# A transformer block on eight cores: the last LayerNorm's apply goes from VectorE to GpSimd, and four weight reads become one

## The chip, the cores and the metric

The kernel runs on 8 cores of one Trainium2 chip. Each core works on one sequence of the batch; nothing is exchanged between cores, and all read their own copy of the same weights. The metric is the device time of the slowest core in microseconds, from a run of the whole kernel. A profile is of one execution; its own time is given beside its span.

## The reference, cut to what matters

```
# per core: x is one sequence, 4096 tokens of 1024
h  = LN(x, g1, b1); spec = h @ W_to.T                # 1024 -> 512
scan over tokens: (sr, si) = clip(rotate(decay*(sr,si) + 0.1*(real,imag)))
x2 = x + 0.1 * (scan_out @ W_from.T)                 # 512 -> 1024
h  = gelu(LN(x2, g3, b3) @ W1.T + b1f)               # 1024 -> 4096
x3 = x2 + 0.1 * (h @ W2.T + b2f)                     # 4096 -> 1024
y  = LN(x + x3)
# eight experts, each token uses the two with the highest router logits
out = LN(y + sum_e c_e * ((silu(y @ G_e.T) * (y @ U_e.T)) @ D_e.T))
```

All LayerNorms are over the 1024 features. The last two have no gain and no bias. Every expert is computed for every token; c_e is zero for those not chosen.

## The kernel before

The data lies transposed: features on the 128 partitions, in KC = 8 chunks, and T = 512 tokens along the row. The sequence is worked in NT = 8 tiles of 512 tokens; `xc(buf, k)` is chunk k of a buffer, 128 x 512. X0 holds the tile's input, X2 the residual stream, ACC the float32 sum of the experts' outputs, BFIN0 and BFIN1 the bf16 inputs of the matmuls.

**Order.** Every engine has one list of instructions that is written out by the Python loops in program order, and it runs it in this order. `w(eng, ms)` puts a wait for a semaphore value into a list; `opi` and `opd` append an instruction or a DMA and return the value that it will raise. VectorE has a drain behind each instruction. SyncE's list holds all the large DMAs: a wait there holds back every DMA behind it.

**Per tile i.** LN3 from X2 (`emit_ln`), feed-forward layer 1 in eight slabs of weights (`emit_ffn1`, matmuls L660), layer 2 in eight slabs (`emit_ffn2`, L693), the LayerNorm to y with `twopass=True`, the router, and then the loop over the eight experts, with four slabs for gate and up (L834) and two for down (L874) each. ACC starts as y, written by GpSimd in eight steps (L458 and L460, `p2_step`) that are strewn over the expert loop, together with the first part (`make_chain`) of tile i + 1.

**The final LayerNorm.** What is done with ACC when the experts are through is a closure, `make_p2`. It isn't run at once, but in `emit_ffn1` of the next tile, behind slab fr = 3; for the last tile it runs at the end. It calls `emit_ln` with ACC: ScalarE casts eight chunks (L408), TensorE sums them with a matrix of ones (L413), ScalarE squares (L417), TensorE sums (L422), VectorE makes MEANT and the variance (L429 to L434), ScalarE takes the root (L436), VectorE the reciprocal into RSTD (L438). Then the apply: for each chunk a subtraction of MEANT (L470, into ZS) and a multiplication with RSTD (L472, back into ACC). Behind it SyncE waits for the last of them (L892) and issues eight output DMAs (L894). MEANT and RSTD are single buffers, which every LayerNorm writes. `st["p2_done"]` is the end of GpSimd's L460 steps, which also read MEANT and RSTD; VectorE waits for it at L432.

**Slabs.** A slab is 128 x 4096 bf16 (1 MB), in one of the four slots of RING (`ring_slot`). In tiles 1 to 7 it is loaded with one DMA from a scratch copy in memory (`emit_slab_load`, L384), as soon as SyncE reaches it and the slot is free. In tile 0 the scratch copy doesn't exist yet. Then `prepass_unit` reads the float32 weights into two slots, 1 MB each (L264), VectorE casts the first half (L295) and ScalarE the second (L293) into a third slot, SyncE waits for both casts and writes the slot to the scratch copy (L299), and TensorE uses the same slot. There are 64 slabs: 8 of w1, 8 of w2, 32 of gate and up, 16 of down. `prepass_unit` also brings in W_to and W_from at the start. Rows of the float32 weights in memory are 16 KB apart for w1T, 4 KB for w2T and dpT and 8 KB for guT; one read takes 2 KB out of each of 128 rows.

Of the kernel before, what the change touches and what calls it, by code (L numbers as in the profile page):

```python
# [8 lines left out]
F32 = mybir.dt.float32  # L9
# [7 lines left out]
KC = D // 128  # L17
# [13 lines left out]
def build(stop_stage="full"):  # L31
# [34 lines left out]
    with es:  # L66
# [14 lines left out]
        G = sb("G", [128, 32 * T], BF16)  # L81
        SG = sb("SG", [128, 8 * T], BF16)
        MEANT = sb("MEANT", [128, T])
        RSTD = sb("RSTD", [128, T])
# [35 lines left out]
        def w(eng, ms):  # L120
            if ms is None:
                return
            if isinstance(ms, list):
                for m in ms:
                    w(eng, m)
                return
            sk, v = ms
            q[eng].append(lambda E, s=sems[sk], vv=v: E.wait_ge(s, vv))
# [28 lines left out]
        bank_free = [None] * 8  # L157
        bank_ready = [None] * 8
# [18 lines left out]
        def slot_dma(j, fn):  # L177
            return opd("sync", "R%d" % j, fn)
# [76 lines left out]
        def prepass_unit(srcs, dst_sb=None, dst_dram=None, scale=None, ncols=2048):  # L255
            halves = []
            for hv in range(len(srcs)):
                jj, slot, msf = ring_slot()
                w("sync", msf)
                g = srcs[hv].shape[0]  # L260
                gc_ = ncols // g
                ms_rd = None
                for gg in range(g):
                    ms_rd = slot_dma(jj, lambda E, d=slot.bitcast(F32)[:, gg * gc_:(gg + 1) * gc_], s=srcs[hv][gg]: E.dma_start(out=d, in_=s))  # L264
                halves.append((jj, slot, ms_rd))
            CENG = (("vector", "V"), ("scalar", "S"))
            if dst_sb is not None:
                ms_cs = []
                for hv, (jj, slot, ms_rd) in enumerate(halves):
                    eng, sk = CENG[hv % 2]  # L270
                    w(eng, ms_rd)
                    dstap = dst_sb[:, hv * ncols:(hv + 1) * ncols]
                    if eng == "scalar":
                        ms_c = opi(eng, sk, lambda E, d=dstap, s=slot.bitcast(F32)[:, 0:ncols], sc=(scale or 1.0): E.activation(out=d, in_=s, func=AF.Copy, scale=sc))
                    elif scale is None:
                        ms_c = opi(eng, sk, lambda E, d=dstap, s=slot.bitcast(F32)[:, 0:ncols]: E.tensor_copy(out=d, in_=s))
                    else:
                        ms_c = opi(eng, sk, lambda E, d=dstap, s=slot.bitcast(F32)[:, 0:ncols], sc=scale: E.tensor_scalar(out=d, in0=s, scalar1=sc, scalar2=None, op0=OP.mult))
                    ring_set_free(jj, ms_c)
                    ms_cs.append(ms_c)  # L280
                return ms_cs, None
            jo, oslot, msfo = ring_slot()
            ms_cs = []
            for hv, (jj, slot, ms_rd) in enumerate(halves):
                eng, sk = CENG[hv % 2]
                w(eng, ms_rd)
                if hv == 0:
                    w(eng, msfo)
                else:
                    w(eng, msfo)  # L290
                dstap = oslot[:, hv * ncols:(hv + 1) * ncols]
                if eng == "scalar":
                    ms_c = opi(eng, sk, lambda E, d=dstap, s=slot.bitcast(F32)[:, 0:ncols]: E.activation(out=d, in_=s, func=AF.Copy))  # L293
                else:
                    ms_c = opi(eng, sk, lambda E, d=dstap, s=slot.bitcast(F32)[:, 0:ncols]: E.tensor_copy(out=d, in_=s))  # L295
                ring_set_free(jj, ms_c)
                ms_cs.append(ms_c)
            w("sync", ms_cs)
            ms_wr = slot_dma(jo, lambda E, d=dst_dram, s=oslot[:]: E.dma_start(out=d, in_=s))  # L299
            return ms_cs, ms_wr, jo, oslot  # L300
# [87 lines left out]

        def emit_ln(src, bfin_p, gv=None, bv=None, dstf=None, out_bf=True,
                    src_ready=None, extra_swait=None, extra_twait=None, extra_vwait=None,  # L390
                    twopass=False):
            BFIN = BFINS[bfin_p]
            per_chunk = isinstance(src_ready, list) and len(src_ready) == KC
            if not per_chunk:
# [4 lines left out]
            sq_ms = [None] * KC  # L399
# [26 lines left out]
            if twopass:  # L426
                bfin_user[bfin_p] = None
            w("vector", bank_ready[0])
            opi("vector", "V", lambda E: E.tensor_scalar(out=MEANT[:], in0=PB[0][:], scalar1=float(1.0 / D), scalar2=None, op0=OP.mult))  # L429
            opi("vector", "V", lambda E: E.tensor_tensor(out=ZS[:, 0:T], in0=MEANT[:], in1=MEANT[:], op=OP.mult))  # L430
            w("vector", bank_ready[1])
            w("vector", st.get("p2_done"))  # L432
            opi("vector", "V", lambda E: E.scalar_tensor_tensor(out=PB[1][:], in0=PB[1][:], scalar=float(1.0 / D), in1=ZS[:, 0:T], op0=OP.mult, op1=OP.subtract))
            ms_veps = opi("vector", "V", lambda E: E.tensor_scalar(out=PB[1][:], in0=PB[1][:], scalar1=float(EPS), scalar2=None, op0=OP.add))  # L434
            w("scalar", ms_veps)
# [7 lines left out]
            if twopass:  # L443
                st["p1_stats"] = ms_pow

                def pass1():
                    for k in range(KC):
                        opi("vector", "V", lambda E, k=k: E.tensor_tensor(out=ZS[:, 0:T], in0=src(k), in1=MEANT[:], op=OP.subtract))
                        bf_ms[k] = opi("vector", "V", lambda E, k=k: E.tensor_tensor(out=xc(BFIN, k), in0=ZS[:, 0:T], in1=RSTD[:], op=OP.mult))  # L449
                    bank_free[0] = bf_ms[KC - 1]  # L450
                    bank_free[1] = bf_ms[KC - 1]
                st["p1_pass1"] = pass1

                def p2_step(k):
                    def go():
                        if k == 0:
                            w("gpsimd", [extra_vwait, bf_ms[KC - 1]])
                        ms_sub = opi("gpsimd", "G", lambda E, k=k: E.tensor_tensor(out=dstf(k), in0=src(k), in1=MEANT[:], op=OP.subtract))  # L458
                        w("gpsimd", ms_sub)
                        f_ms[k] = opi("gpsimd", "G", lambda E, k=k: E.tensor_tensor(out=dstf(k), in0=dstf(k), in1=RSTD[:], op=OP.mult))  # L460
                        st["p2f_%d" % k] = f_ms[k]
                        if k == KC - 1:
                            st["p2_done"] = f_ms[k]
                    return go
                st["p1_pass2_steps"] = [p2_step(k) for k in range(KC)]
                st["p1_sq"] = sq_ms
                return cast_ms, None, sq_ms[KC - 1], bf_ms, f_ms
            w("vector", extra_vwait)
            for k in range(KC):
                opi("vector", "V", lambda E, k=k: E.tensor_tensor(out=ZS[:, 0:T], in0=src(k), in1=MEANT[:], op=OP.subtract))  # L470
# [14 lines left out]
        st = {}  # L485

        def make_chain(j):
# [57 lines left out]
            steps.append(s_ln1a)  # L545

            def s_ln1b():
                w("vector", [bank_ready[0], st.get("p2_done")])
                opi("vector", "V", lambda E: E.tensor_scalar(out=MEANT[:], in0=PB[0][:], scalar1=float(1.0 / D), scalar2=None, op0=OP.mult))
                opi("vector", "V", lambda E: E.tensor_tensor(out=ZS[:, 0:T], in0=MEANT[:], in1=MEANT[:], op=OP.mult))  # L550
                w("vector", bank_ready[1])
                w("vector", st.get("p2_done"))
                opi("vector", "V", lambda E: E.scalar_tensor_tensor(out=PB[1][:], in0=PB[1][:], scalar=float(1.0 / D), in1=ZS[:, 0:T], op0=OP.mult, op1=OP.subtract))
                ms_veps = opi("vector", "V", lambda E: E.tensor_scalar(out=PB[1][:], in0=PB[1][:], scalar1=float(EPS), scalar2=None, op0=OP.add))
                w("scalar", ms_veps)
                ms_sqr = opi("scalar", "S", lambda E: E.activation(out=PB[1][:], in_=PB[1][:], func=AF.Sqrt))
                w("vector", ms_sqr)
                ms_rec = opi("vector", "V", lambda E: E.reciprocal(out=RSTD[:], in_=PB[1][:]))
                bank_free[1] = ms_rec
                ms_pow = ms_rec  # L560
# [156 lines left out]
        for i in range(NT):  # L717
# [170 lines left out]
            def make_p2(i=i, t0=t0, acc_ms=list(acc_ms), gu_ms=last_gu_mm[0]):  # L888
                def p2():
                    _, ms_out, _, _, _ = emit_ln(lambda k: xc(ACC, k), i % 2, dstf=lambda k: xc(ACC, k), out_bf=False,  # L890
                                                 src_ready=acc_ms[KC - 1], extra_swait=gu_ms)
                    w("sync", ms_out)  # L892
                    for k in range(KC):
                        opd("sync", "SO", lambda E, k=k, t0=t0: E.dma_start(out=outTr[k, :, t0:t0 + T], in_=xc(ACC, k)))  # L894
                    prev_out_so[0] = ("SO", cnt["SO"])
                return p2
# [64 lines left out]
```

How the kernel before makes its waits and increments, by code:

```python
        def w(eng, ms):  # L120
            if ms is None:
                return
            if isinstance(ms, list):
                for m in ms:
                    w(eng, m)
                return
            sk, v = ms
            q[eng].append(lambda E, s=sems[sk], vv=v: E.wait_ge(s, vv))
# [8 lines left out]
        def opi(eng, sk, fn):  # L137
            cnt[sk] += STEP[sk]
            v = cnt[sk]
            q[eng].append(lambda E, fn=fn, s=sems[sk], st=STEP[sk]: fn(E).then_inc(s, st))
            if eng in DRAIN_ENGS:
                q[eng].append(lambda E: E.drain())
            return (sk, v)
# [1 line left out]
        def opd(eng, sk, fn):  # L145
            cnt[sk] += STEP[sk]
            v = cnt[sk]
            q[eng].append(lambda E, fn=fn, s=sems[sk], st=STEP[sk]: fn(E).then_inc(s, st))
            return (sk, v)
```

## Time and profile before

| | us |
|---|---|
| runs of the kernel | 5863.69 and 5514.01, median 5688.85 |
| the profiled execution, its own time | 5507.56 |
| its span on the slowest core (core 1) | 5506.0 |
| spans of the eight cores | 5481.4 to 5506.0 |
| TensorE busy (matmuls) | 4188.6, 76% |
| VectorE busy | 1987.8, 36% |
| ScalarE busy | 1045.9, 19% |
| GpSimd busy | 468.8, 9% |
| memory traffic | read 625.09 MB, written 83.89 MB |

Engines are printed as PE (TensorE's matmuls), PEld (its weight loads), DVE (VectorE), ACT (ScalarE), POOL (GpSimd) and SP (SyncE); a q behind a name is its instruction queue, where DMA issues stand. L and a number is a line of the kernel. Times are microseconds from the span's start, the mean of one instruction in ns where it says so. Tile 0 reaches to about 1150 us, the seven others take some 620 us each. What released a waiting instruction is inferred from semaphores: where several were waited for, the one that came last is named.

### The profile page before, as it was taken

How to read it: one execution, taken by the hardware profiler on the slowest of the kernel's cores; microseconds unless marked ns; L12 is line 12 of the kernel's file. 1: busy time of each engine (PE TensorE's matmuls, PEld its weight loads, DVE VectorE, ACT ScalarE, POOL GpSimd, SP SyncE). 2: the span in 40 equal slices, each digit the busy share in tenths (PEclk: the TensorE clock that was granted, in tenths of full speed). 3: DMA queues.
4: the chain of work that ended last, by engine and by line, in shares of the span. 5: the costliest groups of instructions: out<-in, count | busy, mean ns of one | idle time of the engine just before them, and what ended most of it. 6: DMA issues, size and time to landing. Idle time of an engine off the chain costs nothing.

```text
span 5506.0 us, 56606 instructions; the slowest of 8 cores (5481.4 to 5506.0 us)
## 1 busy us (share of the span) xinstructions
PE 4188.6 (76%) x18088; PEld 1776.7 (32%) x18088; DVE 1987.8 (36%) x2937; ACT 1045.9 (19%) x1560; POOL 468.8 (9%) x398
## 2 busy tenths in 40 slices
PE   1365666667899688977899588976899588976897
PEld 0122222223343233433334233433334233433343
DVE  4313442232443235332443235332443235332333
ACT  1122212231111221121101221121201221121111
POOL 0001000000201010100201010100201010100210
PEclk9687888878999789988999789988899789988998
DMA  2265566634233233314233233314234233323342
GB/s 62 66 229 194 201 209 239 238 121 153 107 123 138 84 115 115 138 69 153 107 120 141 82 117 109 143 70 153 100 123 144 80 120 109 138 76 138 115 144 94
DMA packets 178013, 712.66 MB, mean 129 GB/s; under 512 B 28609, under 2 KB 28737, under 8 KB 112194
## 3 DMA queue, kind: packets, MB, share of 16 engines
q1 hardware_dynamic: 168770, 708.95, 36.3%
q8 instruction: 158, 2.59, 0.2%
q10 hardware_dynamic: 8960, 0.10, 0.1%
q14 instruction: 125, 1.02, 0.1%
HBM read 625.09 MB, written 83.89 MB: 129 GB/s over the span
## 4 chain that ended last, share of the span: by engine, by line
PE 63%; DVE 17%; DMA 5%; ACT 5%; SPq 4%; issue 3%; DVEq 1%; ACTq 1%; POOL 0%; POOLq 0%
PE PB L834 28%; PE PB L874 15%; PE PB L660 8%; PE PB L693 7%; SPq L264 3%; DMA RING<-guT 2%; DVE ZS L470 2%; ACT RING L293 2%; DVE RSTD L438 1%; DVE UPE L847 1%; PE PB L633 1%; DVEq L142 1%; DVE PRD L853 1%; DMA RING<-scr_w 1%; PE PB L413 1%
## 5 line engine op out<-in xcount | busy, mean ns | idle before, releaser
L834 PE MATMUL PB<-BFIN,RING 128*128 128x512 bf16 x8192 | 1893.2, 393 | 222.1 <-ACT RING L293 108.8
L834 PEld LDWEIGHTS PB<-BFIN,RING 128*128 128x128 bf16 x8192 | 815.1, 100 | 1280.9 <-issue 392.3
L874 PE MATMUL PB<-PRD,RING 128*128 128x512 bf16 x4096 | 968.6, 399 | 223.3 <-DVE PRD L853 139.9
L660 PE MATMUL PB<-BFIN,RING 128*128 128x512 bf16 x2048 | 514.2, 413 | 440.2 <-DMA RING<-scr_w 225.2
L847 DVE TENSOR_TENSOR UPE<-PB,CBE 128x512 f32<-128x512 f32 x512 | 354.0, 691 | 997.7 <-PE PB L834 960.1
L874 PEld LDWEIGHTS PB<-PRD,RING 128*128 128x128 bf16 x4096 | 411.3, 102 | 775.5 <-issue 351.4
L880 DVE TENSOR_TENSOR ACC<-PB,ACC 128x512 f32<-128x512 f32 x512 | 353.9, 691 | 685.5 <-PE PB L874 666.7
L853 POOL TENSOR_TENSOR PRD<-SG,UPE 128x512 bf16<-128x512 bf16 x256 | 297.1, 1161 | 2799.7 <-DVE UPE L847 2728.2
L841 ACT ACTIVATE SG<-PB 128x512 bf16<-128x512 f32 x512 | 303.6, 597 | 1033.8 <-PE PB L834 1028.0
L693 PE MATMUL PB<-G,RING 128*128 128x512 bf16 x2048 | 465.8, 386 | 21.1 <-ACT RING L293 13.3
L660 PEld LDWEIGHTS PB<-BFIN,RING 128*128 128x128 bf16 x2048 | 211.8, 104 | 741.4 <-issue 539.1
L693 PEld LDWEIGHTS PB<-G,RING 128*128 128x128 bf16 x2048 | 197.5, 99 | 272.6 <-issue 53.8
L703 DVE SCALAR_TENSOR_TENSOR X<-PB,X 128x512 f32<-128x512 f32 x64 | 44.3, 692 | 652.5 <-PE PB L693 652.3
L458 POOL TENSOR_TENSOR ACC<-X,MEANT 128x512 f32<-128x512 f32 x64 | 82.8, 1295 | 2084.4 <-DVE BFIN L449 2084.4
L817 ACT ACTIVATE CBE<-PB 128x512 f32<-128x512 f32 x64 | 38.2, 597 | 1141.8 <-PE PB L814 1140.7
L666 ACT ACTIVATE G<-PB,BHV 128x512 bf16<-128x512 f32 x256 | 175.9, 687 | 276.0 <-PE PB L660 275.7
L853 DVE TENSOR_TENSOR PRD<-SG,UPE 128x512 bf16<-128x512 bf16 x256 | 187.6, 733 | 60.9 <-DVE UPE L847 60.3
L293 ACT ACTIVATE RING<-RING 128x2048 bf16<-128x2048 f32 x64 | 122.2, 1909 | 381.7 <-DMA RING<-dpT 161.8
L295 DVE CAST RING<-RING 128x2048 bf16<-128x2048 f32 x64 | 81.1, 1267 | 297.9 <-DMA RING<-guT 96.0
L408 ACT ACTIVATE BFIN<-X 128x512 bf16<-128x512 f32 x128 | 74.0, 623 | 444.8 <-DVE X L706 394.6
L429 DVE TENSOR_SCALAR MEANT<-PB 128x512 f32<-128x512 f32 x24 | 16.6, 691 | 311.6 <-PE PB L413 311.6
L633 PE MATMUL PB<-ZB,WFR 128*128 128x512 bf16 x256 | 77.3, 431 | 60.5 <-DVE STI L621 51.6
(134 smaller groups left out, 1837.4 us busy)
## 6 DMA issues: line engine op xcount, KB each, us to landing
RING<-scr_gu SPq DMA_DIRECT2D x224, 1024.0 KB, 4.9
RING<-scr_w SPq DMA_DIRECT2D x112, 1024.0 KB, 4.9
RING<-scr_dp SPq DMA_DIRECT2D x112, 1024.0 KB, 4.8
RING<-guT SPq DMA_DIRECT2D x256, 256.0 KB, 5.3
scr_gu<-RING SPq DMA_DIRECT2D x32, 1024.0 KB, 4.9
RING<-dpT SPq DMA_DIRECT2D x128, 256.0 KB, 5.1
X<-xT SPq DMA_DIRECT2D x64, 256.0 KB, 5.3
RING<-w1T SPq DMA_DIRECT2D x64, 256.0 KB, 6.7
```

Of the source, the lines that this page charges most:

```text
L264: ms_rd = slot_dma(jj, lambda E, d=slot.bitcast(F32)[:, gg * gc_:(gg + 1) * gc_], s=srcs[hv][gg]: E.dma_start(out=d, in_=s))
L293: ms_c = opi(eng, sk, lambda E, d=dstap, s=slot.bitcast(F32)[:, 0:ncols]: E.activation(out=d, in_=s, func=AF.Copy))
L633: mmm = opi("tensor", "T", lambda E, c=c, oc=oc: E.matmul(PB[7][:], WFR[:, c * 1024 + oc * 128: c * 1024 + (oc + 1) * 128], xc(ZB, c), sta ...
L660: mmm = opi("tensor", "T", lambda E, k=k, fc4=fc4, b=b, slot=slot: E.matmul(PB[b][:], slot[:, k * 512 + fc4 * 128: k * 512 + (fc4 + 1) * 1 ...
L666: g_ms[fc] = opi("scalar", "S", lambda E, b=b, fc=fc: E.activation(out=xc(G, fc), in_=PB[b][:], func=AF.Gelu, bias=BHV[:, fc:fc + 1]))
L693: mm_last = opi("tensor", "T", lambda E, jx=jx, kr=kr, oc4=oc4, b=b, slot=slot: E.matmul(PB[b][:], slot[:, jx * 512 + oc4 * 128: jx * 512 ...
L834: mmm = opi("tensor", "T", lambda E, k=k, fc4=fc4, b=b, slot=slot, BFIN=BFIN: E.matmul(PB[b][:], slot[:, k * 512 + fc4 * 128: k * 512 + (f ...
L841: sg_ms[gc] = opi("scalar", "S", lambda E, b=b, gc=gc: E.activation(out=xc(SG, gc), in_=PB[b][:], func=AF.Silu))
L847: ms_up = opi("vector", "V", lambda E, b=b, par=par: E.tensor_tensor(out=xc(UPE, par), in0=PB[b][:], in1=CBE[:], op=OP.mult))
L853: prev_upe[par] = opi(peng, psem, lambda E, uc=uc, par=par: E.tensor_tensor(out=xc(PRD, uc), in0=xc(SG, uc), in1=xc(UPE, par), op=OP.mult))
L874: mmm = opi("tensor", "T", lambda E, k=k, oc4=oc4, b=b, slot=slot: E.matmul(PB[b][:], slot[:, k * 512 + oc4 * 128: k * 512 + (oc4 + 1) * 1 ...
L880: acc_ms[oc] = opi("vector", "V", lambda E, oc=oc, b=b: E.tensor_tensor(out=xc(ACC, oc), in0=PB[b][:], in1=xc(ACC, oc), op=OP.add))
```

## The change

Two things are changed. In `prepass_unit`, the g reads of 128 rows x 2 KB of one half become a single DMA whose access patterns have three levels: partition, row block k, column. Bytes, source, destination and slot are the same, and the semaphore is waited for at the value of one DMA in place of g. g is 4, for W_from 2.

In `emit_ln` there is a new path, `apply_gp`, which only the final LayerNorm takes. GpSimd waits for the reciprocal and then does subtraction and multiplication of the eight chunks in place in ACC, each multiplication behind a wait for its own subtraction. Its end is kept as `pl2_done`, and VectorE waits for it, and for `p2_done`, ahead of each new MEANT; the wait for `p2_done` that stood ahead of L433 is now ahead of L429.

```diff
@@ prepass_unit
-                ms_rd = None
-                for gg in range(g):
-                    ms_rd = slot_dma(jj, lambda E, d=slot.bitcast(F32)[:, gg * gc_:(gg + 1) * gc_], s=srcs[hv][gg]: E.dma_start(out=d, in_=s))
+                dview = slot.bitcast(F32)[:, 0:ncols].rearrange("p (k f) -> p k f", k=g)
+                sview = srcs[hv].rearrange("k p f -> p k f")
+                ms_rd = slot_dma(jj, lambda E, d=dview, s=sview: E.dma_start(out=d, in_=s))
@@ emit_ln
             w("vector", bank_ready[0])
+            w("vector", [st.get("p2_done"), st.get("pl2_done")])
             opi("vector", "V", lambda E: E.tensor_scalar(out=MEANT[:], ...
             opi("vector", "V", lambda E: E.tensor_tensor(out=ZS[:, 0:T], ...
             w("vector", bank_ready[1])
-            w("vector", st.get("p2_done"))
...
+            if apply_gp:
+                w("gpsimd", [ms_rec, extra_vwait])
+                for k in range(KC):
+                    m1 = opi("gpsimd", "G", lambda E, k=k: E.tensor_tensor(out=dstf(k), in0=src(k), in1=MEANT[:], op=OP.subtract))
+                    w("gpsimd", m1)
+                    f_ms[k] = opi("gpsimd", "G", lambda E, k=k: E.tensor_tensor(out=dstf(k), in0=dstf(k), in1=RSTD[:], op=OP.mult))
+                st["pl2_done"] = f_ms[KC - 1]
+                bank_free[0] = f_ms[KC - 1]
+                bank_free[1] = f_ms[KC - 1]
+                return None, f_ms[KC - 1], sq_ms[KC - 1], bf_ms, f_ms
@@ s_ln1b, the first LayerNorm of the next tile
-                w("vector", [bank_ready[0], st.get("p2_done")])
+                w("vector", [bank_ready[0], st.get("p2_done"), st.get("pl2_done")])
@@ make_p2
-                                                 src_ready=acc_ms[KC - 1], extra_swait=gu_ms)
+                                                 src_ready=acc_ms[KC - 1], extra_swait=gu_ms, apply_gp=True)
```

## Rows read from the trace of the kernel before

**Rows 1.** The chain that ended last: shares by engine (page), by line

```profile
PE 63%; DVE 17%; DMA 5%; ACT 5%; SPq 4%; issue 3%; DVEq 1%; ACTq 1%; POOL 0%; POOLq 0%
...
by line: PE PB L834 28.4%; PE PB L874 14.9%; PE PB L660 7.6%; PE PB L693 7.2%; SPq L264 3.4%; issue 3.4%; DMA RING<-guT 2.4%; DVE ZS L470 1.6%; ACT RING L293 1.6%; DVE RSTD L438 1.5%; DVE UPE L847 1.2%; PE PB L633 1.1%; DVEq L142 1.1%; DVE 
```

**Rows 2.** Waits of TensorE and SyncE's queue: total us, times, longest

```profile
PE PB L660 <- DMA RING<-scr_w: 225.2, 7, 34.5
...
SPq L128 <- DVE ACC L472: 686.2, 8, 90.2
```

**Rows 3.** Timeline, tile 1: start us, us, engine, line, out<-in, count [idle]

```profile
1188.01 28.92 PE L660 MATMUL PB<-BFIN,RING 128*128 128x512 bf16 x121 [1.62 <-DVE BFIN L477]
...
1232.06 3.36 DVE L438 RECIPROCAL RSTD<-PB 128x512 f32<-128x512 f32 x1 [2.05 <-ACT PB L436]
1235.51 0.69 DVE L470 TENSOR_TENSOR ZS<-ACC,MEANT 128x512 f32<-128x512 f32 x1
...
1247.27 0.69 DVE L472 TENSOR_TENSOR ACC<-ZS,RSTD 128x512 f32<-128x512 f32 x1
1248.03 4.46 SPq L894 DMA_DIRECT2D outT<-ACC  x8
1252.59 67.86 SPq L384 DMA_DIRECT2D RING<-scr_w  x12
...
1260.88 29.85 PE L660 MATMUL PB<-BFIN,RING 128*128 128x512 bf16 x128 [32.54 <-DMA RING<-scr_w]
```

**Rows 4.** Timeline of GpSimd, tile 1's expert loop

```profile
1413.89 1.52 POOL L460 TENSOR_TENSOR ACC<-ACC,RSTD 128x512 f32<-128x512 f32 x1
1415.38 1.26 POOL L458 TENSOR_TENSOR ACC<-X,MEANT 128x512 f32<-128x512 f32 x1
...
1423.28 1.28 POOL L458 TENSOR_TENSOR ACC<-X,MEANT 128x512 f32<-128x512 f32 x1
1424.70 1.27 POOL L460 TENSOR_TENSOR ACC<-ACC,RSTD 128x512 f32<-128x512 f32 x1
```

**Rows 5.** GpSimd's L458: count, shortest/median/longest ns, first and last start

```profile
L458 POOL TENSOR_TENSOR ACC<-X,MEANT x64: 1256/1264/2244, 488.0 to 5150.4; 128x512 f32<-128x512 f32 x64
```

**Rows 6.** Timeline of one slab's cycle in tile 0

```profile
859.93 0.33 SPq L299 DMA_DIRECT2D scr_gu<-RING  x1
...
860.25 7.07 PE L834 MATMUL PB<-BFIN,RING 128*128 128x512 bf16 x32 [2.83 <-DVE RING L295]
860.41 4.80 SPq L264 DMA_DIRECT2D RING<-guT  x8
...
870.65 1.91 ACT L293 ACTIVATE RING<-RING 128x2048 bf16<-128x2048 f32 x1 [10.87 <-DMA RING<-guT]
872.63 0.33 SPq L299 DMA_DIRECT2D scr_gu<-RING  x1
```

**Rows 7.** Timeline of the end of the program

```profile
5482.59 3.36 DVE L438 RECIPROCAL RSTD<-PB 128x512 f32<-128x512 f32 x1 [2.05 <-ACT PB L436]
...
5497.79 0.69 DVE L472 TENSOR_TENSOR ACC<-ZS,RSTD 128x512 f32<-128x512 f32 x1
```

**Rows 8.** Timeline of tile 1: the next writer of MEANT

```profile
1353.81 0.69 DVE L429 TENSOR_SCALAR MEANT<-PB 128x512 f32<-128x512 f32 x1 [2.86 <-PE PB L413]
```

**Rows 9.** Windows: us, busy by engine, PEclk, DMA share, GB/s

```profile
861.40:870.60 9.20, 5.92 (x28) 2.47 (x26) 5.34 (x7) 0.00 (x0) 2.32 (x2) 1.00 0.90 308
870.60:874.00 3.40, 1.19 (x3) 0.43 (x4) 0.03 (x1) 1.91 (x1) 0.00 (x0) 0.79 0.18 77
```

**Rows 10.** SyncE's issues of L264 for guT: shortest/median/longest ns

```profile
L264 SPq DMA_DIRECT2D RING<-guT x256: 327/436/2612, 460.9 to 1115.3; - x128
```

**Rows 11.** Timeline of SyncE, tile 0: writes that end a slab's cycle

```profile
232.66 0.33 SPq L299 DMA_DIRECT2D scr_w<-RING  x1
...
340.94 0.33 SPq L299 DMA_DIRECT2D scr_w<-RING  x1
...
442.75 0.33 SPq L299 DMA_DIRECT2D scr_w<-RING  x1
```

More of the change, by code:

```diff
@@ L390, in emit_ln @@
                     src_ready=None, extra_swait=None, extra_twait=None, extra_vwait=None,
-                    twopass=False):
+                    twopass=False, apply_gp=False):
             BFIN = BFINS[bfin_p]
```

## Prediction

> **What bounds the kernel now.** I read the page's chain first. The chain of work that ended last is 63% TensorE, 17% VectorE, 5% DMA and 4% SyncE's queue, with line 264, one of the two edited places, at 3.4% [rows 1]. So TensorE's matmuls set the end wherever they run without a gap, and an edit pays or costs only where TensorE stands idle. Then I read who waited for whom. One wait of TensorE is tied to the other edit: in the first feed-forward layer (L660) it waits 225.2 us for a slab from the scratch copy, 7 times, 34.5 us at the longest; and SyncE's queue waits 686.2 us, 8 times, for L472, the last instruction of the final LayerNorm's apply [rows 2]. Seven is the number of tiles after the first, and eight adds the end of the program.
>
> The timeline of one of these stalls shows its whole length as one series [rows 3]. TensorE's matmuls of slab 3 end at 1188.01 + 28.92 = 1216.93. ScalarE casts ACC, TensorE sums, ScalarE squares, VectorE takes mean and reciprocal (ends 1232.06 + 3.36 = 1235.42). VectorE applies, 16 instructions from 1235.51 to 1247.96. SyncE, which stood in its order at the wait for the last of them, issues the eight output DMAs at 1248.03 (4.46 us), and only then, at 1252.59, the load of slab 4, which TensorE needs and gets at 1260.88. The profile prints the last 8 us as a DMA wait, but what it holds back is the order of SyncE's queue: every microsecond that the apply takes longer, the slab comes later, and TensorE has nothing else.
>
> Tile 0 is another regime. There each slab is read as float32, cast by two engines and written back, and a cycle of SyncE takes 872.63 - 859.93 = 12.70 us, while the 32 matmuls of a slab take 7.07 [rows 6]. So in tile 0 the load cycle is the bound.
>
> **Change, part 1: the apply goes from VectorE to GpSimd.** Removed are 16 VectorE instructions per tile (L470 and L472), one pair per 1.57 us: 12.45 us from first start to last end [rows 3]. Added are the same 16 on GpSimd, each pair tied by a wait of GpSimd for itself. The trace has this very pair, in float32 on the same shapes: L458 and L460, 64 each. One instruction takes 1264 ns in the median, 1256 at the least [rows 5]. From the pair that starts at 1415.38 to the one at 1423.28 are three periods of 2.63 us, semaphore included [rows 4]. Eight pairs take 7 x 2.63 + (1424.70 + 1.27 - 1423.28) = 21.1 us. The difference is 21.1 - 12.45 = 8.65 us per apply; I take 8.7. Lower bound: every instruction at the minimum, 16 x 8 ns less, 8.5. Upper bound: one multiply took 1.52 us in place of 1.27 [rows 4] while VectorE worked beside it; if all eight did, 2 us more. VectorE has nothing to do in this stretch, so I leave that out.
>
> How much of it is on the path? All of it in seven tiles, by the series above: 7 x 8.7 = 60.9. The eighth apply is the end of the program: the reciprocal ends at 5485.95 and the last multiply at 5498.48, 12.5 us as in the stall [rows 3, 7], and behind it come only the output DMAs. There another 8.7 us lands on the end. Sum of part 1: 8 x 8.7 = +69.6 us.
>
> What does VectorE gain with its 12.45 us free? Its next instruction is the residual add L703, which waits for TensorE's matmuls of the second layer; nothing queued on VectorE behind the apply is late, so the gain is 0. ScalarE's part (cast, squares, root) is untouched. The waits moved and added ahead of MEANT cost nothing. The moved one is for GpSimd's pass over ACC in the expert loop, which ends at 1425.97 in tile 1 [rows 4], while the next final LayerNorm comes only with the next tile. The new one is for the end of the apply, 1247.96 + 8.7 = 1256.7, and the next writer of MEANT starts at 1353.81 [rows 8]: 97 us of cover (that writer too moves back with the stall). Without the cover, VectorE's statistics and all behind them would wait for as long as GpSimd is late. GpSimd itself has no work queued between: its next instruction is the first subtraction of the expert loop, after that writer.
>
> **Change, part 2: four reads of 256 KB become one of 1 MB.** It touches 12 DMAs of the prologue, which become 4, and 8 reads per slab, which become 2, in 64 slabs of tile 0: 512 issues become 128. The tempting sum is this: eight issues take 4.80 us of a 12.70 us cycle [rows 6], and the chain gives L264 3.4% of 5506 = 187 us [rows 1]. But look at what the DMA engines do meanwhile. From 861.4 to 870.6 they are busy 90% and move 308 GB/s; from 870.6 until 874 they have next to nothing [rows 9]. The issues (860.41 to 865.21) lie inside that busy stretch. The lone issue of the write takes 0.33 us; guT's median is 0.436 and the maximum 2.6 [rows 6, 10]: the longer ones are SyncE waiting for room, not work. The last read ends about 5.4 us after the last issue. What follows the transfer, ScalarE's 1.91 us cast, the issue of the write at 872.63 and the start of the next transfer, is not touched. So the price of the 8 issues is hidden under the transfers, and I take 0 us.
>
> Bounds, since no DMA of this trace has four 2 KB runs per partition. Gain: if the boundaries between eight DMAs cause the missing 10% of the busy stretch, 0.92 us per slab, 64 x 0.92 = 59 us. Loss: the reads then step through memory in another order; a partition's four runs lie 128 rows apart. The only row that shows order or pitch to matter is w1T: its seven cycles from 232.66 to 340.94 take 15.5 us each, the eight of w2T from 340.94 to 442.75 take 12.7 (108.28 / 7 and 101.81 / 8) [rows 11], with the rows of w1T 16 KB apart and those of w2T 4 KB. If the 56 other slabs fell to w1T's pace: 56 x 2.74 = +153 us.
>
> The Trainium skill (page "DMA: Bandwidth & Descriptors", section "Bandwidth") says to batch transfers to 1 MiB or more, and its anatomy section gives each a fixed 2 us. An estimate by that page, with four serial transfers of 256 KB against one, (2.6 us each by its fit) against one of 4.4, would save 6 us per half-slab and some 770 us in all. That is the mechanism of rival A below, at another size. The trace disagrees in the premise: queued transfers overlap, at 308 GB/s [rows 9].
>
> **Sum.** 0 + 69.6 on the profiled execution's 5507.56 gives 5577 us. That execution is near the faster of the two runs shown (5514.01); their median, 5688.85, is pulled up by the other (5863.69), and I don't start from it.
>
> **Rivals.**
> A, faster: the issues are the bound of tile 0. If L264's whole share of the chain goes, 5577 - 187 = 5390, 2.1% below 5507.56. It decides only if more than 69.6 us goes, 1.1 us per slab, and that much is more than the 0.92 us in which the engines are not full. For it: the chain's share. Against it: rows 9. Chance 0.07.
> B, slower by more: the merged reads run slower. At the bound above: 5577 + 153 = 5730 (5620 to 5800 if a quarter of it comes, or half as much again). It counts as slower over 2% from +41 us, that is 0.64 us per slab. For it: w1T's pace; against it: the same rows are read, 2 KB at a time. Chance 0.20.
> The Trainium skill (same page, section "Latency and other measured facts") has copies at row pitches of 512 KiB, 2 MiB and 4 MiB at 207, 164 and 103 GB/s, which would speak for B, as the four runs lie 0.5 to 2 MiB apart; no row here shows such a pitch.
> C, no change: the longer apply is hidden, because SyncE's wait is not what delays slab 4. Then 5507 (5490 to 5520). It would need slab 4 loaded before; the issue at 1252.59 says no. Chance 0.04.
> The forecast has 0.69, with its own range 5518 (full gain of part 2) to 5600.
>
> **Range and chances.** 5515 to 5730: the forecast's range and most of B. Two per cent, about what a measurement of this kernel can tell from no change, is 110 us. Faster 0.06; within 2% 0.71; slower 0.23 (B and a little of the forecast's upper end).
>
> **What would show it.** In the profile after: GpSimd has 128 more float32 tensor instructions and VectorE 128 fewer; TensorE's wait for the scratch slab in L660 grows from 225 to about 286 us, seven stalls of some 41 us; SyncE waits for GpSimd's last multiply; the last 21 us before the output DMAs are GpSimd's. In tile 0 L264 has 132 issues, its share of the chain falls and that of the DMAs takes its place, and the cycle stays at 12.7 us. The prediction is wrong if that cycle moves by over 0.6 us, or if the pairs on GpSimd don't take 2.6 us each.

## The result, and the profile after

| | kernel before | changed kernel |
|---|---|---|
| median of all runs | 5701.98 us (42 runs) | 5619.54 us (43 runs) |
| lowest run | 5505.41 us | 5550.32 us |
| profiled execution, slowest core | 5506.0 us | 5543.2 us |
| profiled execution, mean of the eight cores | 5494.3 us | 5535.0 us |
| ratio to the kernel before | | 1.0068, 95% interval 1.0045 to 1.0091 |

Both kernels have executions in which some cores run at a lower clock and the time is up to 600 us longer, and the plain medians mix them in; the ratio is made without them. The change makes the kernel slower by 0.7%, some 37 us, less than 2%.

The page of the changed kernel, its span and the chain of work that ended last, shares by engine and by line:

```profile
span 5543.2 us, 55832 instructions; the slowest of 8 cores (5526.5 to 5543.2 us)
...
PE 61%; DVE 16%; DMA 8%; ACT 5%; issue 4%; POOL 3%; DVEq 1%; SPq 1%; ACTq 1%; POOLq 0%
PE PB L844 28%; PE PB L884 15%; PE PB L670 8%; PE PB L703 7%; DMA RING<-guT 3%; ACT RING L293 2%; DVE RSTD L438 1%; POOL ACC L473 1%; POOL ACC L471 1%; DMA RING<-w2T 1%; DMA RING<-dpT 1%; DVE UPE L857 1%; DMA RING<-w1T 1%; DVE PRD L863 1%; PE PB L643 1%
```

The issues of L264 (3.4% before [rows 1]) are no longer among the lines listed and SyncE's queue is at 1%; the DMAs' share has risen from 5% to 8%, and GpSimd, at 0% before, holds 3% with the two lines of the new apply. The waits that answer to [rows 2] (total us, times, longest), of TensorE and of SyncE's queue:

```profile
PE PB L670 <- DMA RING<-scr_w: 288.5, 7, 42.1
```

```profile
SPq L128 <- POOL ACC L473: 750.9, 8, 98.8
```

225.2 us have become 288.5, over the same seven stalls: 9.0 us more each. The stall in tile 1, in the timeline (start us, us, engine, line, operation):

```profile
1198.94 3.36 DVE L438 RECIPROCAL RSTD<-PB 128x512 f32<-128x512 f32 x1 [2.05 <-ACT PB L436]
1202.44 1.26 POOL L471 TENSOR_TENSOR ACC<-ACC,MEANT 128x512 f32<-128x512 f32 x1 [100.44 <-DVE RSTD L438]
1203.85 1.26 POOL L473 TENSOR_TENSOR ACC<-ACC,RSTD 128x512 f32<-128x512 f32 x1
1205.07 1.26 POOL L471 TENSOR_TENSOR ACC<-ACC,MEANT 128x512 f32<-128x512 f32 x1
...
1222.21 1.26 POOL L473 TENSOR_TENSOR ACC<-ACC,RSTD 128x512 f32<-128x512 f32 x1
1223.54 4.46 SPq L904 DMA_DIRECT2D outT<-ACC  x8
1228.10 69.23 SPq L384 DMA_DIRECT2D RING<-scr_w  x12
...
1237.43 30.18 PE L670 MATMUL PB<-BFIN,RING 128*128 128x512 bf16 x125 [42.14 <-DMA RING<-scr_w]
```

The reciprocal ends at 1202.30 and the sixteen instructions run from 1202.44 to 1223.47: 21.0 us, in pairs 2.62 to 2.63 us apart (1202.44, 1205.07). Output DMAs, slab load and restart follow as they did before, and TensorE's stall is 42.14 us in place of 32.54 [rows 3], of which 1.0 is a slower landing of this one slab (9.33 us from issue to restart, 8.29 before). The same sixteen at the end of the program:

```profile
5514.70 1.26 POOL L471 TENSOR_TENSOR ACC<-ACC,MEANT 128x512 f32<-128x512 f32 x1 [33.43 <-DVE RSTD L438]
...
5534.46 1.26 POOL L473 TENSOR_TENSOR ACC<-ACC,RSTD 128x512 f32<-128x512 f32 x1
5535.79 4.47 SPq L904 DMA_DIRECT2D outT<-ACC  x8
```

Tile 0 is where the other part of the change shows. SyncE's timeline, the writes to the scratch copy that end w1T's and w2T's cycles, as in [rows 11], and the last write of the tile:

```profile
233.81 0.34 SPq L299 DMA_DIRECT2D scr_w<-RING  x1
234.24 1.48 SPq L264 DMA_DIRECT2D RING<-w1T  x2
...
329.38 0.34 SPq L299 DMA_DIRECT2D scr_w<-RING  x1
...
431.84 0.34 SPq L299 DMA_DIRECT2D scr_w<-RING  x1
```

```profile
1117.63 0.34 SPq L299 DMA_DIRECT2D scr_dp<-RING  x1
1118.12 7.19 SPq L384 DMA_DIRECT2D RING<-scr_w  x4
```

Two issues take 1.48 us here, where eight took 4.80 [rows 6], and the issues of guT have 367 ns at the least and 592 in the median:

```profile
L264 SPq DMA_DIRECT2D RING<-guT x64: 367/592/1416, 448.0 to 1080.6; - x64
```

The eight cycles of w2T take 12.8 us where they took 12.7, but the seven of w1T take 13.7 in place of 15.5 (means of the eight cores: 12.9 in place of 13.8), and the tile's last write stands at 1117.63 us where the core shown before had it at 1149.26. A window of one cycle's transfers and the pause behind it (busy us by engine, granted clock, DMA share, GB/s):

```profile
825.40:834.40 9.00, 6.73 (x32) 2.84 (x29) 1.80 (x2) 2.39 (x4) 0.00 (x0) 1.00 0.92 320
834.40:838.00 3.60, 1.37 (x4) 0.58 (x5) 0.12 (x1) 1.91 (x1) 0.00 (x0) 0.74 0.25 102
```

The engines are a little fuller in the stretch, 92% and 320 GB/s against 90% and 308 [rows 9]. Over the slabs of tile 0 on all eight cores, the DMA records give more than these two windows: from the first to the last packet of a slab's 1024 reads 6.23 us in place of 6.83, the pause behind it 4.06 in place of 3.96, the whole cycle 13.53 in place of 13.85. A slab's reads get 0.6 us shorter, and half of that is given back before the first read (0.2 us) and in the pause (0.1 us).

The 37 us between the two slowest cores add up from these rows, though the even sum is in part the luck of these two cores. Up to the first output DMA the changed kernel is 1248.03 - 1223.54 = 24.5 us ahead: 31.6 us gained by the end of tile 0, 8.8 lost in the first stall, 1.7 gained around it. From the first output DMA to the last one's issue it takes 5535.79 - 1223.54 = 4312.25 us, against 5498.55 - 1248.03 = 4250.52: 61.7 us more, seven applies (six stalls and the end) at 8.8 us. 61.7 - 24.5 = 37.2, the difference of the spans. In the mean of the eight cores the difference is 40.7 us and is made up otherwise: the last write of tile 0 comes 19.7 us earlier (1137.2 and 1117.5), from there to the first output DMA takes 10.7 us more, and the seven periods behind it 49.6 us more (4253.3 and 4302.9), 7.1 each. So the apply costs 60 us in this pair and not 70, and the merged reads give back 20 and not 32.

### The profile page after: what moved, and what is told of

Same layout as the page of the kernel before. It is cut to its first block, busy times and chain, and to the rows that moved or that the text cites. A ratio compares the mean times of both kernels' runs of the same rounds, so it can differ in the third digit from the quotient of the medians.

```text
span 5543.2 us, 55832 instructions; the slowest of 8 cores (5526.5 to 5543.2 us)
## 1 busy us (share of the span) xinstructions
PE 4147.0 (75%) x17736; PEld 1772.7 (32%) x18088; DVE 1899.6 (34%) x2809; ACT 1045.7 (19%) x1560; POOL 627.8 (11%) x526
## 4 chain that ended last, share of the span: by engine, by line
PE 61%; DVE 16%; DMA 8%; ACT 5%; issue 4%; POOL 3%; DVEq 1%; SPq 1%; ACTq 1%; POOLq 0%
PE PB L844 28%; PE PB L884 15%; PE PB L670 8%; PE PB L703 7%; DMA RING<-guT 3%; ACT RING L293 2%; DVE RSTD L438 1%; POOL ACC L473 1%; POOL ACC L471 1%; DMA RING<-w2T 1%; DMA RING<-dpT 1%; DVE UPE L857 1%; DMA RING<-w1T 1%; DVE PRD L863 1%; PE PB L643 1%
## 5 line engine op out<-in xcount | busy, mean ns | idle before, releaser
L844 PE MATMUL PB<-BFIN,RING 128*128 128x512 bf16 x8024 | 1871.3, 392 | 226.5 <-ACT RING L293 93.5
L670 PE MATMUL PB<-BFIN,RING 128*128 128x512 bf16 x2001 | 506.8, 411 | 494.8 <-DMA RING<-scr_w 288.5
L827 ACT ACTIVATE CBE<-PB 128x512 f32<-128x512 f32 x64 | 38.2, 597 | 1141.7 <-PE PB L824 1140.6
L458 POOL TENSOR_TENSOR ACC<-X,MEANT 128x512 f32<-128x512 f32 x64 | 82.8, 1294 | 1329.4 <-DVE BFIN L449 1329.4
L471 POOL TENSOR_TENSOR ACC<-ACC,MEANT 128x512 f32<-128x512 f32 x64 | 80.7, 1261 | 685.8 <-DVE RSTD L438 685.8
```

The source lines that it names most:

```text
L471: m1 = opi("gpsimd", "G", lambda E, k=k: E.tensor_tensor(out=dstf(k), in0=src(k), in1=MEANT[:], op=OP.subtract))
L670: mmm = opi("tensor", "T", lambda E, k=k, fc4=fc4, b=b, slot=slot: E.matmul(PB[b][:], slot[:, k * 512 + fc4 * 128: k * 512 + (fc4 + 1) * 1 ...
L844: mmm = opi("tensor", "T", lambda E, k=k, fc4=fc4, b=b, slot=slot, BFIN=BFIN: E.matmul(PB[b][:], slot[:, k * 512 + fc4 * 128: k * 512 + (f ...
```

## The experiments

The runs of one group shared a chip and the runs of the kernel before. Since tile 0 varies from core to core (before: last write to the scratch copy between 1124 and 1149 us), I give the mean over the eight cores for it. That mean is also given for some whole kernels, beside the ratio of the slowest cores.

**1. Each part alone.** First the apply on GpSimd with the old reads:

```diff
 (changed kernel)
-                dview = slot.bitcast(F32)[:, 0:ncols].rearrange("p (k f) -> p k f", k=g)
-                sview = srcs[hv].rearrange("k p f -> p k f")
-                ms_rd = slot_dma(jj, lambda E, d=dview, s=sview: E.dma_start(out=d, in_=s))
+                for gg in range(g):
+                    ms_rd = slot_dma(jj, ... one read of 256 KB, as before)
```

> The final LayerNorm's apply on GpSimd, the reads of tile 0 as four of 256 KB. Theory (the apply lies on the path in all eight places, and the merged reads gave back the rest): the seven stalls of TensorE in the first feed-forward layer take 41 to 42 us each, the time rises by 8 x 8.7 = 70 us, 1.013 of the kernel before, and tile 0 is as before (mean cycle of an expert slab 14.0 us, last write to the scratch copy near 1137 us in the mean of the cores). Rival (the apply costs less than its own length and the reads gave nothing): some 37 us, 1.007.

Measured: 1.0151 of the kernel before, interval 1.0084 to 1.0218. The forecast's 1.013 lies in it, the rival's 1.007 does not (the interval is wide). The expectation for tile 0 failed: its last write came at 1160.3 us in the mean of the cores, not near 1137, and its slabs' cycle was 14.2 us. TensorE's stalls are those of the changed kernel:

```profile
PE PB L670 <- DMA RING<-scr_w: 289.8, 7, 42.0
```

Then the merged reads alone:

```diff
 (kernel before)
-                for gg in range(g):
-                    ms_rd = slot_dma(...)
+                dview = slot.bitcast(F32)[:, 0:ncols].rearrange("p (k f) -> p k f", k=g)
+                sview = srcs[hv].rearrange("k p f -> p k f")
+                ms_rd = slot_dma(jj, lambda E, d=dview, s=sview: E.dma_start(out=d, in_=s))
```

> The merged reads alone, the apply on VectorE. Theory: tile 0 gets some 20 to 30 us shorter (expert slab cycle 13.75 us in place of 14.0), the stalls stay at 32.5 us, 0.995 of the kernel before. Rival (the reads gave nothing, tile 0 of the changed kernel was a lucky draw): 1.000, cycle 14.0 us.

Measured: 0.998, interval 0.9938 to 1.0022, which holds both expectations. The mean over the eight cores is 5489 us against 5508 for the kernel before, 19 us less. The stalls are the old ones:

```profile
PE PB L660 <- DMA RING<-scr_w: 222.5, 7, 32.3
```

The ratio alone doesn't settle this part; tile 0 of all the kernels (experiment 2) and experiment 3 do.

**2. How many DMAs per half.** Two reads of 512 KB (`srcs[hv][gg:gg + 2]` into two row blocks at a time, four DMAs per slab):

> The apply on VectorE, and each half of a slab read with two DMAs of 512 KB (4 per slab). Theory (each DMA of the stream leaves a small gap, so the time goes with their count): 4 gaps fewer than before, 2 more than with one read per half, so two thirds of the gain: slab cycle near 13.85 us, 0.9965. Rival (it is the order of the reads in memory, four runs per partition): about half or none of it.

Measured: 1.0012, interval 0.997 to 1.0053. The theory's 0.9965 lies just outside, and the mean over the cores, 5509 us against 5508, shows no gain either, so by the time the rival is favoured; the cycle of an expert slab in its trace is between the others' (below). Eight reads of 64 partitions, sixteen DMAs per slab:

```diff
+                    for hp in range(2):
+                        ms_rd = slot_dma(jj, lambda E, d=slot.bitcast(F32)[hp * 64:(hp + 1) * 64, gg * gc_:(gg + 1) * gc_], s=srcs[hv][gg][hp * 64:(hp + 1) * 64]: E.dma_start(out=d, in_=s))
```

> The apply on VectorE, and each half read with eight DMAs of 64 partitions x 2 KB (16 per slab). Theory (the time goes with the count of DMAs, 0.05 to 0.1 us each): 8 more per slab, cycle of an expert slab 14.0 + 0.4 to 0.8 us, 25 to 50 us in all, 1.005 to 1.009. Rival (the count does not matter, the order in memory does; a read still takes 2 KB of each row): 1.000. Third: SyncE's issues, at least 0.33 us each, become the bound: 16 x 0.33 = 5.3 us is still under the 6 us of transfer, so no more than the theory's figure.

Measured: 1.0374, interval 1.0316 to 1.0432, four times what any theory gave. One cycle on SyncE, then the issues of guT (shortest, median and longest ns), then the transfers' window:

```profile
862.97 0.33 SPq L300 DMA_DIRECT2D scr_gu<-RING  x1
863.44 11.03 SPq L265 DMA_DIRECT2D RING<-guT  x16
879.99 0.33 SPq L300 DMA_DIRECT2D scr_gu<-RING  x1
```

```profile
L265 SPq DMA_DIRECT2D RING<-guT x512: 465/597/2448, 507.8 to 1313.2; - x171
```

```profile
864.50:877.00 12.50, 8.38 (x33) 3.31 (x32) 1.92 (x2) 2.39 (x4) 0.00 (x0) 0.90 0.86 220
```

The cycle is 17.0 us. The sixteen issues take 11.03 us, at 465 ns for the shortest and 597 for the median, while the engines move 220 GB/s at a share of 0.86. So it is not only the issues that are dear: by the DMA records each engine spends 8.5 us in the packets of a slab's reads against 5.6 to 6.2 in the others, for the same bytes. In this form the packets themselves are slower, so it can't speak for the count of DMAs, and the expectation was wrong on both counts.

The last write of tile 0, mean of the eight cores, profiled executions:

| | four reads per half | two | one |
|---|---|---|---|
| the pair under study | 1137.2 (before) | | 1117.5 (changed) |
| first group | 1160.3 (apply on GpSimd) | 1144.9 | 1134.7 |
| last group (experiments 4 and 5) | 1140.0, 1141.7 | | 1124.6, 1126.5 |

Three pairs of four reads against one: 20, 26 and 15 us. Single kernels of one form differ by up to 23 us from chip to chip (1137 to 1160), as much as the effect. The DMA records of the same profiles separate the forms better (us per slab of tile 0, means over 62 slabs on each of eight cores; the read stretch is the time from the first to the last packet of the slab's reads):

| | four reads per half | two | one |
|---|---|---|---|
| read stretch | 6.83 (before), 7.26, 6.88, 6.93 | 6.83 | 6.23 (changed), 6.49, 6.30, 6.35 |
| cycle | 13.85 (before), 14.20, 13.89, 13.92 | 13.94 | 13.53 (changed), 13.78, 13.62, 13.67 |

With one read the cycle is 0.26 to 0.42 us shorter within a group, 17 to 27 us for 64 slabs. Two reads stand between the two forms of their group (7.26 and 6.49; 14.20 and 13.78). But the eight cycles of w2T are 13.2 us with two reads and 12.7 to 12.9 in the other kernels of the table; why is not shown.

**3. The load cycle in all eight tiles.** To lift the effect over that spread, the condition that takes the scratch copy is switched off, so that every tile reads and casts the float32 weights, 512 slabs in place of 64:

```diff
-            if key not in scr_ready:
+            if True:
```

Four reads per half:

> To make tile 0's load cycle large against the spread between runs, every tile reads the float32 weights again and writes the scratch copy again, as tile 0 does (512 slabs in place of 64); four reads per half, apply on VectorE. Both theories: some 7 x 300 us more than the kernel before, near 7600 us, mean cycle of a slab 14.0 us. It is the base of the next three.

One read per half:

> As the kernel that reads the weights in every tile, with one read per half. Theory (the merged reads fill gaps of the read stretch, 0.3 to 0.5 us per slab): 512 slabs, 150 to 250 us less than with four reads. Rival (no gain, tile 0 of the changed kernel was luck): within 30 us of it.

Two reads per half:

> As the kernel that reads the weights in every tile, with two reads per half. Theory (gain by count of DMAs): two thirds of the gain of one read. Rival (gain from the four runs of a partition in one DMA): a third or less. No gain at all would fit what this form showed in tile 0 alone, w2 cycles of 13.1 us against 12.8.

One read per half, a partition's four runs in neighbouring rows (`rearrange("(p k) f -> p k f", k=4)` in place of blocks of 128 rows). This kernel doesn't put the weights' rows back in order, so its output isn't the reference's; it serves for the time alone:

> As the one with one read per half in every tile, but partition p takes the four neighbouring rows 4p to 4p + 3 and not four rows that lie 128 rows apart, so the weights' rows are permuted and the output is not the reference's. Theory (only the count of DMAs matters): as with one read per half, within 50 us. Rival (the distance of a partition's runs in memory costs time, the forecast's case B): it is faster, by over 100 us.

| | median of 4 runs (lowest, highest) | slab cycle | read stretch | pause behind it |
|---|---|---|---|---|
| four reads | 8287 us (8158, 8360) | 14.15 us | 6.97 us | 4.12 us |
| two reads | 8117 us (8059, 8210) | 13.69 us | 6.54 us | 3.90 us |
| one read | 8131 us (8001, 8202) | 13.55 us | 6.37 us | 3.95 us |
| one read, neighbouring rows | 8059 us (8000, 8114) | 13.54 us | 6.39 us | 4.06 us |

Cycle (first packet of one write to first packet of the next), read stretch (first to last packet of the 1024 reads) and pause are means over the 489 slabs on each of eight cores with exactly 1024 reads and a cycle under 30 us, from the DMA records. The total was misjudged, 7600 us expected, since I took 300 us per tile more where it was 370 or more. In the profile with four reads TensorE's mean granted clock was 0.73, in the others 0.80, so the cycles and pauses of the first row can't be held against the others; I rely on the read stretch, in which TensorE has no part: it is shorter by 0.60 us with one read and by 0.43 with two, and no core of one group reaches into the other (6.77 to 7.28 with four, 6.22 to 6.52 with one). The pages and one window over 600 to 7800 us show the same from outside, the rates with the clocks mixed in (0.74 in the window with four reads, 0.79 and 0.80 in the others). Four reads per half:

```profile
DMA packets 694178, 1653.00 MB, mean 199 GB/s; under 512 B 85953, under 2 KB 86081, under 8 KB 628290
```

```profile
600.00:7800.00 7200.00, 4528.63 (x15654) 1751.86 (x15965) 2205.82 (x2829) 1655.71 (x1746) 424.99 (x339) 0.74 0.61 202
```

One read per half:

```profile
DMA packets 644874, 1652.60 MB, mean 207 GB/s; under 512 B 36673, under 2 KB 36801, under 8 KB 579010
```

```profile
600.00:7800.00 7200.00, 4468.23 (x16689) 1762.40 (x16690) 2281.61 (x2918) 1716.44 (x1798) 443.26 (x354) 0.80 0.62 212
```

Two reads, then neighbouring rows:

```profile
600.00:7800.00 7200.00, 4415.37 (x16214) 1754.11 (x16537) 2266.72 (x2898) 1703.74 (x1787) 438.49 (x350) 0.80 0.62 210
```

```profile
600.00:7800.00 7200.00, 4512.82 (x16379) 1782.58 (x16705) 2281.18 (x2920) 1714.04 (x1798) 443.09 (x354) 0.79 0.60 212
```

The packets under 512 B fall from 85953 to 36673, by 49280 = 16 x 3080: 3080 DMAs fewer, each with 16 small packets besides its data. The rate goes from 202 GB/s to 210 with two reads and 212 with one. What a slab gains is better read from cores at like clocks. Taking from all runs the halves of the chip (cores 0 to 3, 4 to 7) whose clock was 0.79 or more, the kernel with four reads needs 8109 us (clock 0.795), with two 8011 (0.801), with one 7937 (0.805). That is 172 us or 0.34 us per slab with one read, 0.19 with two; the lowest runs, 8158 and 8001 us, give 0.31. The 150 to 250 us expected of one read came; two reads gave 98, over half of it, near the two thirds of the theory. For the 64 slabs of the real kernel it makes 20 to 22 us, as tile 0 showed. Neighbouring rows change nothing, 13.54 against 13.55: the distance of a partition's runs in memory costs nothing here.

**4. Is the stall SyncE's order?** The wait for the apply and the output DMAs move behind the load of the fourth slab of the second feed-forward layer:

```diff
-                    w("sync", ms_out)
-                    for k in range(KC):
-                        opd("sync", "SO", ...)
-                    prev_out_so[0] = ("SO", cnt["SO"])
+                    def outs():
+                        w("sync", ms_out)
+                        ... the same eight DMAs
+                    pending_out[0] = outs
@@ emit_ffn2, behind emit_slab_load
+                    if fr == 0 and kr == 3 and pending_out[0] is not None:
+                        pending_out[0](); pending_out[0] = None
```

On the kernel before:

> The kernel before, but SyncE's wait for the apply and the eight output DMAs stand behind the load of the fourth slab of the second feed-forward layer, no longer ahead of slab 4 of the first. Theory (the stall is SyncE's order, not the arithmetic): slab 4 is loaded long before; TensorE goes on right behind the sums of squares, at 1228.3 in place of 1260.9 in the timeline, 32.5 us less in each of seven tiles, 228 us, 0.959. Rival (the LayerNorm's own work on VectorE and ScalarE holds TensorE back): 0.99 or more.

Measured: 0.9554, interval 0.9493 to 0.9614. The timeline around the LayerNorm in tile 1:

```profile
1197.17 59.54 SPq L384 DMA_DIRECT2D RING<-scr_w  x8
...
1226.26 2.43 PE L422 MATMUL PB<-BFIN,ONESB 128*128 128x512 bf16 x8
...
1228.53 27.79 PE L660 MATMUL PB<-BFIN,RING 128*128 128x512 bf16 x128
...
1232.42 3.36 DVE L438 RECIPROCAL RSTD<-PB 128x512 f32<-128x512 f32 x1 [2.06 <-ACT PB L436]
...
1247.62 0.69 DVE L472 TENSOR_TENSOR ACC<-ZS,RSTD 128x512 f32<-128x512 f32 x1
...
1256.83 4.90 SPq L900 DMA_DIRECT2D outT<-ACC  x8
```

TensorE goes from the sum of squares into slab 4 with no pause at all, at 1228.53, while VectorE is still ahead of the apply; the output DMAs follow at 1256.83. The stall of 32.5 us was SyncE's order and nothing else. The gain is some 245 us (213 to 279), the seven stalls and 17 us more; where these come from is not shown, but the mean granted clock of the profiled cores rose from 0.88 to 0.90.

On the changed kernel:

> The changed kernel (apply on GpSimd, one read per half) with the same later place of the output DMAs. Theory (the apply on GpSimd costs only because SyncE waits for it): seven of the eight extra 8.7 us are hidden, only the one at the end of the program stays, so 9 us slower than the next kernel, about 0.956 of the kernel before. Rival (GpSimd's apply slows other engines or is waited for elsewhere): 60 us or more slower than the next kernel.

Measured: 0.9513, interval 0.9463 to 0.9562. With one read and the apply on VectorE:

> One read per half, the apply on VectorE, and the output DMAs in the later place: the combination that should beat both kernels. Theory: 228 us by the stalls and 20 to 30 us by tile 0, 0.954 to 0.956 of the kernel before. Rival (with TensorE busier, the granted clock or the loads give part of it back): 0.97.

Measured: 0.9507, interval 0.9466 to 0.9547, the fastest of all, 5269.7 us in the median. Once SyncE doesn't wait, it hardly matters which engine applies: the mean spans are 5253.7 us (GpSimd) and 5249.9 (VectorE), 3.8 apart where 9 were expected, and where the apply on GpSimd had cost some 60 before.

**5. The apply shared.** GpSimd takes chunks 0 to 2, VectorE 3 to 7, at once:

```diff
-                for k in range(KC):
+                for k in range(3):
                     m1 = opi("gpsimd", ...)
...
+                for k in range(3, KC):
+                    opi("vector", "V", ... subtract into ZS)
+                    f_ms[k] = opi("vector", "V", ... multiply into ACC)
```

> The kernel before with the apply shared: GpSimd does chunks 0 to 2, VectorE 3 to 7 at the same time; four reads, output DMAs in the old place. Theory (the path takes the longer of the two, no more): max(3 x 2.63, 5 x 1.57) = 7.9 us in place of 12.5, 4.6 us less in eight places, 37 us, 0.993. Rival (the two engines slow each other on shared memory ports): pairs of over 2 us on VectorE, 1.000 or slower.

Measured: 1.0011, interval 0.997 to 1.0052. The rival was right. The timeline:

```profile
1254.01 1.76 POOL L471 TENSOR_TENSOR ACC<-ACC,MEANT 128x512 f32<-128x512 f32 x1 [105.01 <-DVE RSTD L438]
1254.74 1.57 DVE L478 TENSOR_TENSOR ACC<-ZS,RSTD 128x512 f32<-128x512 f32 x1
1255.91 1.52 POOL L473 TENSOR_TENSOR ACC<-ACC,RSTD 128x512 f32<-128x512 f32 x1
1256.41 1.57 DVE L477 TENSOR_TENSOR ZS<-ACC,MEANT 128x512 f32<-128x512 f32 x1
...
1263.07 1.57 DVE L477 TENSOR_TENSOR ZS<-ACC,MEANT 128x512 f32<-128x512 f32 x1
1264.74 0.69 DVE L478 TENSOR_TENSOR ACC<-ZS,RSTD 128x512 f32<-128x512 f32 x1
...
1266.31 0.69 DVE L478 TENSOR_TENSOR ACC<-ZS,RSTD 128x512 f32<-128x512 f32 x1
1267.09 4.46 SPq L908 DMA_DIRECT2D outT<-ACC  x8
```

With both engines at float32 operands in SBUF, a VectorE instruction takes 1.57 us in place of 0.69 and GpSimd's 1.52 to 1.76 in place of 1.26. The apply lasts from 1253.96 to 1267.00, 13.0 us, longer than VectorE's 12.45 alone. The Trainium skill ("GPSIMD Engine Reference", section "Specifications") says that GpSimd's SBUF interfaces are shared with VectorE, with contention for VectorE instructions of two SBUF inputs; this trace agrees, at a factor of 2.3 for VectorE.

## Why the prediction came out as it did

**The bound in tiles 1 to 7.** Right. The series through SyncE's queue, read from one timeline, was the whole stall: with the later output DMAs TensorE doesn't pause there at all. (That it goes on at 1228.53, with 1228.3 expected, is luck, for the two timelines are of different cores, whose tile 0 ends up to 25 us apart.)

**Part 1.** Right in place, and nearly in size: 8.7 us per apply forecast, 8.8 in the seven periods of the two slowest cores, pairs of 2.63 us, seven stalls (288.5 us where some 286 were forecast) and the end; alone it gave 1.0151 with 1.013 inside the interval. But not every microsecond of a longer stall reaches the end, as the prediction had it: in the mean of the eight cores the periods grew by 7.1 us and the whole part costs 60 us in place of 70. What gives the 10 us back is not shown. The bound that a VectorE instruction beside it would make GpSimd slower was rightly left out of the sum, for VectorE stands idle in this stretch; experiment 5 shows what it costs otherwise.

**Part 2.** Here the step failed: "So the price of the 8 issues is hidden under the transfers, and I take 0 us." The first half stands: the eight issues, 187 us by their share of the chain, became two and gave only a small part of it, so rival A didn't come. But the price of a DMA boundary inside the transfers was not 0. The missing 10% of the busy stretch was the right place, named as a bound of 0.92 us per slab and 59 us, and the runs give some 0.3 us and 20 us, a third of the bound: 19.7 us in the pair of profiled kernels (mean of the cores), 19 us with the reads alone, 20 to 22 us by experiment 3. I had rows for both ends and chose an end. With the measured 20 us the sum would have been 70 - 20 = +50 us; the 10 us that part 1 gave back make it +40, as in the mean of the cores (40.7), and the measured ratio is +37 (25 to 50). The expected sign of being wrong, a cycle that moves by over 0.6 us, did not come; it was set too wide, for 0.3 us per slab already made 20 us. The cycle's level, 12.7 us, was one row's; the mean is 13.85 before and 13.53 after. The estimate of 770 us had another reason to fail besides the overlap: the page of the Trainium skill gives its 2 us for DMAs that GpSimd issues, and these are SyncE's.

**The size of the whole.** +70 us (1.3%) was forecast on the profiled execution, +37 us (0.7%) measured: the direction held, the size was about twice too large. The changed kernel's median of 5619.54 us lies inside 5515 to 5730, and the time stayed within 2%, the likeliest of the three. But the number 5577 stands on the profiled execution, and it is 112 us below the median of 5688.85 that was shown for the kernel before, so beside that median it reads as a gain of 2%, the wrong way. The forecast should have been given as a ratio to the time that it starts from, and set against that median too.

**Rival B** (the merged reads run slower) is false, and its evidence was misread. The 15.5 us per cycle of w1T was one core's; over the eight cores before it ranges from 12.4 to 15.5 with the same 16 KB rows, so the pitch alone doesn't make it; their mean, 13.8, is still 1.0 above w2T's, and why is open. Neighbouring rows against rows 128 apart settle what B needs: no difference. The Trainium skill ("DMA: Bandwidth & Descriptors", section "Latency and other measured facts") has copies between tensors in memory fall from 207 to 103 GB/s as the row pitch grows from 512 KiB to 4 MiB. That has no counterpart in these reads, which move 212 GB/s over the window whether a partition's 2 KB runs lie 0.5 to 2 MiB apart or in neighbouring rows.

**Rival C** (the apply is hidden) is false for the change as it is, and becomes true with the output DMAs moved.

**What stays open.** What in a DMA's end costs the 0.1 us is not shown: the 16 small packets, the start of the next DMA, or SyncE's issues. Going from eight DMAs per slab to four took 0.43 us off the read stretch, from four to two 0.17, some 0.1 us for each DMA less, so a fixed price per DMA fits but isn't proved: in the real kernel two reads per half gained nothing in time. The form with 64 partitions per DMA, meant to tell, changed something else.

## What to carry to other kernels

A wait in the queue that issues the DMAs delays every later load: before moving arithmetic from one engine to another, look at whether its end gates that queue, and move the output DMAs behind the loads that don't depend on it. That was worth 4.5% here, where the choice of engine was worth 1.5% (0.8 to 2.2). A share of the chain that issues hold is little gain if the DMA engines are nearly full meanwhile, but part of the time in which they are not full can be won, so put a value between the bounds and not at one. And read a stage on all cores before a pair of its rows is taken for a rule or two cores' spans for a sum.

## What the runs showed of the hardware that was not expected

- VectorE and GpSimd on float32 tensor-tensor work at the same time: 1.57 us against 0.69 for VectorE, 1.52 to 1.76 against 1.26 for GpSimd. Sharing the work three to five gained nothing (13.0 us against 12.45).
- A read of 64 partitions x 2 KB costs SyncE at least 465 ns of issue, one of 128 partitions x 2 KB 327, one of 128 partitions x 4 x 2 KB 367. Sixteen of the small ones per slab lengthened the cycle from some 14 to 17 us, and the time in their packets from some 6 to 8.5 us per engine.
- Four times fewer DMAs for the same 2 MB in the same 2 KB runs shorten the read stretch from 6.97 to 6.37 us; in the real kernel the cycle keeps half of that, 0.3 us.
